# Low parts of the first twelve weight pieces: from GpSimd and VectorE to identity matmuls and ScalarE copies

## The reference, cut to what matters

```python
def _L0_xattn_ref(h, adj_raw, Wq, Wk, gamma_raw):      # h: context, adj_raw: layernorm(x)
    Q = (h @ Wq.T).reshape(b, n, H, d).transpose(0, 2, 1, 3)
    K = (h @ Wk.T).reshape(b, n, H, d).transpose(0, 2, 1, 3)
    sim = jnp.einsum('bhnd,bhmd->bnm', Q, K) / (jnp.sqrt(jnp.float32(d)) * H)
    k = max(1, int(n * TOP_K_RATIO))
    threshold = jax.lax.top_k(sim, k)[0][:, :, -1:]
    A_learned = jax.nn.sigmoid(sim) * (sim >= threshold)
    A_learned = (A_learned + jnp.swapaxes(A_learned, -1, -2)) * 0.5
    gamma = jax.nn.sigmoid(gamma_raw)
    return (1.0 - gamma) * adj_raw + gamma * A_learned
...
x = x + jnp.tanh(g_xattn[0]) * _L0_xattn_ref(ctx_512, _layernorm(x), Wq, Wk, gamma_raw)
xf = _layernorm(x).reshape(-1, C)
y, g = jnp.split(xf @ shared_gw.T, 2, axis=-1)
shared = jax.nn.silu(g) * y @ shared_dw.T
...
x = x + jnp.tanh(g_ffn[0]) * (shared + out)
```

## Time and profile before

| | us |
|---|---|
| median of 3 runs | 598.53 (596.35 to 601.9) |
| profiled execution, its own time | 597.36 |
| its span, first to last instruction | 595.3 |
| mean granted clock of TensorE | 0.937 of full |
| busy: TensorE, VectorE, ScalarE, GpSimd | 505.0, 343.4, 262.7, 231.9 |

### The profile page before, as it was taken

One profiled execution on the slowest core, in us unless ns is written; L12 is line 12 of the kernel. 1 busy time (PEld: TensorE's weight loads), 2 busy tenths in 40 slices (PEclk: granted clock), 3 DMA queues, 4 the chain that ended last, 5 costly groups with the idle time before them and its releaser, 6 DMA issues.

```text
span 595.3 us, 11124 instructions
## 1 busy us (share of the span) xinstructions
PE 505.0 (85%) x3169; PEld 287.2 (48%) x3170; DVE 343.4 (58%) x708; ACT 262.7 (44%) x473; POOL 231.9 (39%) x226
## 2 busy tenths in 40 slices
PE   2302588889998999879998799999999999999992
PEld 0100344444443454444464356666666666666661
DVE  0589758787868786977964477433333333333331
ACT  0696588646774678433231255322322222222221
POOL 1147735462446334540223034344344343343322
PEclk9955779989999999987999899999999999999997
DMA  3236293215610561054005778535435445445433
GB/s 114 95 93 185 78 305 94 57 41 187 237 45 29 169 248 50 29 186 166 0 1 165 235 230 210 95 73 87 91 71 89 88 72 91 84 73 96 77 40 49
DMA packets 33200, 65.84 MB, mean 111 GB/s; under 512 B 4176, under 2 KB 4432, under 8 KB 33168
## 3 DMA queue, kind: packets, MB, share of 16 engines
q1 hardware_dynamic: 24432, 44.99, 23.2%
q0 software_dynamic: 8736, 20.45, 19.1%
HBM read 42.10 MB, written 23.33 MB: 110 GB/s over the span
## 4 chain that ended last, share of the span: by engine, by line
PE 58%; DVE 18%; ACT 7%; issue 6%; DMA 6%; POOL 2%; SPq 1%; DVEq 1%; POOLq 0%; ACTq 0%
PE py L1006 12%; PE pg L986 12%; PE pu L987 12%; PE pg L848 5%; PE pu L848 5%; PE pt_bank L807 4%; DVE w L1180 3%; DVE pa L1139 3%; DVE w L1110 2%; PE pa L996 2%; PE pu L865 2%; DVE w L1143 1%; ACT w L619 1%; DVE w L1187 1%; ACT w L613 1%
## 5 line engine op out<-in xcount | busy, mean ns | idle before, releaser
L986 PE MATMUL pg<-w,x_t 128*128 x468 | 141.9, 315 | 3.8 <-DVE x_t L1442 3.8
L987 PE MATMUL pu<-w,x_t 128*128 x468 | 141.9, 315 | 0.0
L541 POOL DMA_INDIRECT out<-rows,idx x39 | 61.8, 1584 | 138.0 <-ACT rows L747 134.0
L1006 PE MATMUL py<-w,work 128*128 x351 | 82.1, 379 | 0.8 <-DVE work L1437 0.8
L848 PE MATMUL pg<-w 128*128 128x512 f16 (+1 forms) x288 | 79.9, 387 | 2.6 <-DVE work L1233 2.6
L848 PE MATMUL pu<-w 128*128 128x512 f16 (+1 forms) x288 | 79.5, 386 | 0.0
L737 ACT ACTIVATE work<-pg 128x352 f32<-128x352 f32 x39 | 18.1, 463 | 132.5 <-PE pu L987 132.5
L580 ACT ACTIVATE w<-stage 128x544 f16<-128x544 f32 (+1 forms) x80 | 51.0, 647 | 38.8 <-DMA stage<-in_weights 38.4
L488 POOL TENSOR_TENSOR w<-stage,w 128x544 f16<-128x544 f32 (+1 forms) x43 | 53.4, 1250 | 27.4 <-ACT stage L584 25.6
L494 POOL TENSOR_TENSOR work<-work 128x512 f16<-128x512 f32 (+1 forms) x24 | 29.0, 1208 | 81.8 <-ACT work L649 81.8
L1426 DVE SCALAR_TENSOR_TENSOR work<-pu,work 128x352 f32<-128x352 f32 x39 | 20.5, 525 | 65.4 <-ACT work L737 65.4
(11 more groups left out here) (187 smaller groups left out, 756.5 us busy)
## 6 DMA issues: line engine op xcount, KB each, us to landing
stage<-in_weights SPq DMA_DIRECT2D x80, 272.0 KB, 3.6
out<-rows SPq DMA_DIRECT2D x17, 256.0 KB, 5.3
w<-in_x SPq DMA_DIRECT2D x4, 1024.0 KB, 6.8
out<-w SPq DMA_DIRECT2D x16, 256.0 KB, 3.1
xn_rows<-w SPq DMA_DIRECT2D x16, 256.0 KB, 5.5
rows<-out SPq DMA_DIRECT2D x16, 256.0 KB, 2.8
w<-in_ctx_t SPq DMA_DIRECT2D x4, 256.0 KB, 3.6
out<-rows,idx POOLq DMA_INDIRECT x39, 4.8
```

What stands on the lines that cost most here:

```text
L541: pool.indirect_dma_start(out=out, out_offset=bass.IndirectOffsetOnAxis(ap=idx[:, t:t + 1], axis=0), in_=rows[:, t % 2, :], in_offset=None ...
L986: pe.matmul(pg[p][:, 0:H], lhs, w[:, item, half, at:at + H], start=begin, stop=end)
L987: mm = pe.matmul(pu[p][:, 0:H], lhs, w[:, item, half, at + H:at + 2 * H], start=begin, stop=end)
L1006: mm = pe.matmul(py[:, :], hid_t[:, p, part * JC + j, :], w[:, item, half, at:at + C], start=(j, part, half) == (0, 0, 0), stop=(j, part) ...
```

## The change

Low parts of pieces 0 to 11 are made by TensorE: for each half of a piece (272 columns) an fp32 matmul of a diagonal matrix of 256 with the staged fp32, less an fp16 matmul of the identity with the high part, summed in one of four PSUM banks. ScalarE copies each half out as the fp16 low part, and so releases the stage buffer; it no longer scales those pieces in place. Low parts from piece 12 on in items 0 to 2 are all GpSimd's (VectorE makes none of them), and they stand later in its order. TensorE's ten first low parts come ahead of `missed_rows(0)`, the two last behind the projection of batch 1. ScalarE's pieces 16 and 17 lie between the copies of q and k and the normalised rows. TensorE's single wait for the first 16 pieces becomes waits in front of the shared pieces and the down products that read them. Cut to its core:

```diff
+BY_PE = 12
+        low_banks = [py, pu[0], pt_bank, pg[0]]
+        HALF_W = CHUNK_W // 2
...
         def by_dve(item, n):
-            if not isinstance(item, int):
-                return False
-            if item >= LATE:
-                return True
-            return n % RING == RING - 1 and (item >= EARLY - 1 or item * CHUNKS + n < BY_DVE)
+            return isinstance(item, int) and item >= LATE
+
+        def by_pe(item, n):
+            return isinstance(item, int) and item * CHUNKS + n < BY_PE
...
@@ GpSimd
+            c.mark(pool.memset(scaled_ident[:], 0.0))
+            c.mark(pool.memset(minus_ident[:], 0.0))
...
-            for m in (ident, ident16):
+            for m, one in ((ident, 1.0), (ident16, 1.0), (scaled_ident, W_SCALE), (minus_ident, -1.0)):
...
-            first_pieces(0, FIRST)
             add_attention(0)
-            first_pieces(FIRST, FIRST + 3)
+            first_pieces(BY_PE, BY_PE + 1)
             row_scalars(0)
-            first_pieces(FIRST + 3, FIRST + 6)
+            first_pieces(BY_PE + 1, BY_PE + 4)
             guess(1)
             o.clear()
-            first_pieces(FIRST + 6, BEFORE * CHUNKS)
+            first_pieces(BY_PE + 4, BEFORE * CHUNKS)
...
@@ ScalarE
-                if not by_dve(item, n):
+                if not by_dve(item, n) and not by_pe(item, n):
                     after(act, w_hi, item * CHUNKS + n + 1)
                     act.activation(stage[:, n % RING, :], stage[:, n % RING, :], ACT.Copy, scale=W_SCALE).then_inc(w_scaled, 1)
+            def low_from_bank(k):
+                at = k % CHUNKS * CHUNK_W
+                for half in range(2):
+                    after(act, low_mm, k * 2 + half + 1)
+                    act.activation(w[:, k // CHUNKS, 1, at + half * HALF_W:at + (half + 1) * HALF_W],
+                                   low_banks[(k * 2 + half) % 4][:, 0:HALF_W], ACT.Copy).then_inc(w_lo[k % RING] if half else low_sb, 1)
...
-                high_piece(n // CHUNKS, n % CHUNKS)
+                high_piece(0, n)
+                if n >= 2:
+                    low_from_bank(n - 2)
             base(0, (TPB - 1,))
-            for k in range(ROUNDS, FIRST + RING):
+            for k in range(ROUNDS, BY_PE):
+                low_from_bank(k - 2)
                 high_piece(k // CHUNKS, k % CHUNKS)
-            scores_and_rows(0, True, range(FIRST + RING, FIRST + RING + 2))
-            for k in range(FIRST + RING + 2, BEFORE * CHUNKS):
+            for k in range(BY_PE - 2, BY_PE):
+                low_from_bank(k)
+            for k in range(BY_PE, HALVES * CHUNKS):
+                high_piece(k // CHUNKS, k % CHUNKS)
+            scores_and_rows(0, True, range(HALVES * CHUNKS, HALVES * CHUNKS + 2))
+            for k in range(HALVES * CHUNKS + 2, BEFORE * CHUNKS):
                 high_piece(k // CHUNKS, k % CHUNKS)
...
@@ TensorE
+            def low_pieces(begin, end):
+                for k in range(begin, end):
+                    at = k % CHUNKS * CHUNK_W
+                    after(pe, w_hi, k + 1)
+                    for half in range(2):
+                        bank_, lo, hi = low_banks[(k * 2 + half) % 4], half * HALF_W, (half + 1) * HALF_W
+                        if k >= 2:
+                            if half:
+                                after(pe, w_lo[(k - 2) % RING], (k - 2) // RING + 1)
+                            else:
+                                after(pe, low_sb, k - 1)
+                        pe.matmul(bank_[:, 0:HALF_W], scaled_ident[:], stage[:, k % RING, lo:hi], start=True, stop=False)
+                        pe.matmul(bank_[:, 0:HALF_W], minus_ident[:], w[:, k // CHUNKS, 0, at + lo:at + hi],
+                                  start=False, stop=True).then_inc(low_mm, 1)
+            def pieces_ready(n):
+                for r_, s in enumerate(w_lo):
+                    after(pe, s, len(range(r_, n, RING)))
+                after(pe, w_hi, n)
...
+                if 0 in ks and off == 0:
+                    pieces_ready(half * CHUNKS + -(-UP_W // CHUNK_W))
...
+                if 0 in pieces and i == 0:
+                    pieces_ready(HALVES * CHUNKS)
...
             pe.wait_ge(const_ok, 2)
+            low_pieces(0, BY_PE - 2)
             missed_rows(0)
             project(1, None)
+            low_pieces(BY_PE - 2, BY_PE)
+            after(pe, w_lo[(BY_PE - 1) % RING], (BY_PE - 1) // RING + 1)
             turn_attention(0)
             for i in range(TPB):
                 scores(1, i)
             for i in range(TPB):
                 turn_batch(0, i)
-            for s in w_lo:
-                after(pe, s, HALVES * (CHUNKS // RING))
-            after(pe, w_hi, HALVES * CHUNKS)
...
```

More of the change, by code:

```diff
@@ L19 @@
 BEFORE = 3
-FIRST = 14
-BY_DVE = 20
+BY_PE = 12
 KEEP = int(SEQ * 0.3)
@@ L129, in build @@
         ident, ident16 = sb("ident", [P, P]), sb("ident16", [P, P], F16)
+        scaled_ident, minus_ident = sb("scaled_ident", [P, P]), sb("minus_ident", [P, P], F16)
         ones, tri = sb("ones", [P, P], F16), sb("tri", [P, P], F16)
@@ L206, in build @@
         w_scaled = sem("w_scaled")
+        low_mm, low_sb = sem("low_mm"), sem("low_sb")
         x_ld, ctx_ld = sem("x_ld"), sem("ctx_ld")
@@ L253, in scaled_pieces @@
         def scaled_pieces(item, n):
[L254 to L257, removed]
+            return item * CHUNKS + n + 1 - BY_PE
         ROWS_DVE = BATCHES * (TPB - 1)
@@ L428, in _ @@
             c.wait()
-            for m in (ident, ident16):
-                c.mark(pool.affine_select(out=m[:], in_=m[:], compare_op=ALU.not_equal, fill=1.0, base=0,
+            for m, one in ((ident, 1.0), (ident16, 1.0), (scaled_ident, W_SCALE), (minus_ident, -1.0)):
+                c.mark(pool.affine_select(out=m[:], in_=m[:], compare_op=ALU.not_equal, fill=one, base=0,
                                           pattern=[[-1, P]], channel_multiplier=1))
@@ L1153, in count_missed, with masks @@
                 o.then(dve.tensor_reduce(thr[:], hot8, AX.X, ALU.add))
-            def masks(b, piece=None):
+            def masks(b):
                 after(dve, miss_mm, b + 1)
                 o.then(dve.tensor_copy(missed_i[:], pa[0][0:1, 0:1]))
-                if piece is not None:
-                    low_piece(*piece)
                 any_missed = dve.value_load(missed_i[0:1, 0:1], min_val=0, max_val=P * TPB)
@@ L1201, in attended @@
                 dve.sem_inc(ln_stats, 1)
-                if shared is None:
-                    low_piece(HALVES, 3)
                 if shared is not None:
@@ L1248, in _ @@
                 search(0, n)
-            low_piece(0, 3)
             thresholds(0, (0, 1))
-            low_piece(0, 7)
             thresholds(0, (2, 3))
             count_missed()
-            masks(0, (1, 3))
-            low_piece(1, 7)
+            masks(0)
             attended(0, True, None)
```

## The result

The changed kernel takes 612.61 us (median of 4, 610.11 to 613.73), the kernel before 598.72; the ratio is 1.0219, 95% interval 1.0185 to 1.0253. The page: busy shares and the granted clock in 40 slices.

A forecast was written before the change was run, and what follows sets the result against it. TensorE's gap-free start was taken as the bound, set by GpSimd's low part 18 through SP's queue to batch 1's x. 13.5 + 1.8 + 0.2 = 15.5 on 597.4 gave 612.9, 614 on the median; 8-in-10 range 606 to 621.

The forecast's parts named there:

- (b): Count rounds on VectorE: first L1139 at 40.3 instead of 42.67, four cost 2.7 not 5.7, missed count ready near 47.
- (c): TensorE's ten low parts precede the missed-rows matmul, 2.4 each at half clock, 1.2 at full; matmul at 51.5, 2.0 earlier.
- (d): Missed rows to statistics of attended tiles: 2.2 gained without VectorE's low parts; masks stay 5.7, statistics at 64.1.
- (e): ScalarE's pieces 16 and 17 precede normalised rows, load 17 waits for low part 13: rows at 71.5, 1.1 lost.
- (f): GpSimd's low part 18 falls behind batch 1's guess, 13.7 later; x at 100.7, TensorE resumes at 107.3, 13.5 later.
- (g): TensorE idles some 14 us behind batch 0's first two shared pieces, then restarts at half clock, costing 1.8 (0 to 2.5).
- (h): Readiness waits before TensorE's shared pieces and first down group, 60 in four batches: 0.2.
- From there all as before, only shifted: After TensorE's idle stretch and half-clock restart in batch 0, the remaining timeline is unchanged except for the shift.
- the first: Rival: TensorE's clock doesn't rise during the head's low parts; missed rows at 56.7, everything 5 later, 619; chance 0.18.
- The second: Rival: same order, smaller; stores and x take 11, masks 2 shorter, restart free; 9 slower, 607.5; chance 0.17.
- The third: Rival: faster; early counts help, batch 1's x load isn't held, TensorE starts about 4 sooner, 594.5; chance 0.08.
- the fourth: Rival: order as forecast, but slack makes up the delay of batch 1 to within 1%; chance 0.07.

The follow-up runs named there:

- e5: Changed kernel with TensorE's readiness waits put back to one set for 16 pieces ahead of batch 0's router product; 612.26 us, ratio 1.0220.
- e7_unrolled: Changed kernel with TensorE's loop over batches 0 and 1 written out, same work; 612.09 us, ratio 1.0214.
- e7_warm: Changed kernel with TensorE's loop written out and 58 unused matmuls filling its gap behind shared piece 1 of batch 0; 612.94 us, ratio 1.0230.
- e2: Changed kernel with ScalarE's pieces 16 and 17 moved behind the normalised rows and scores of batch 1; 608.06 us, ratio 1.0152.
- e1: Changed kernel with SP's weight loads 20 to 22 moved behind batch 0's stores and the load of batch 1's x; 600.96 us, ratio 1.0022.
- e6: Kernel before the change with SP's weight loads 20 to 22 moved behind the load of batch 1's x; 599.84 us, ratio 1.0022.
- e12: Changed kernel, queues reordered, one wait set, missed rows behind eight low parts, tile stores behind load 16, row stores behind loads 22 and 23; 593.68 us, ratio 0.9914.
- e8: Changed kernel with loads 20 to 22 behind x, ScalarE's pieces 16 and 17 behind the rows, and one set of readiness waits; 597.61 us, ratio 0.9973.
- e3: Changed kernel with loads 20 to 22 behind the load of x and ScalarE's pieces 16 and 17 behind the rows; 599.20 us, ratio 1.0009.
- e9: Changed kernel with SP, ScalarE and GpSimd orders laid out anew (x ahead of row stores and loads 22, 23) and one wait set; 597.73 us, ratio 0.9983.

## Why the prediction was right

The forecast was 614 and 612.6 was measured; the steps behind it can be laid beside the trace. The agreement is good to about 1 us and not to a few tenths: the four profiles that share the change's queues (the changed kernel, e5, e7_unrolled and e7_warm) have TensorE resume at 106.46 to 108.25.

(a) Constants: nothing, as said. The head of this profiled execution is 1.4 late at VectorE's first count all the same (29.86 against 28.48). The load ahead of it and the first scores' clock differ, other runs of the same head lie on both sides (first statistics of x between 24.0 and 26.5), so I take it for chance.

(b) Count rounds: first L1177 at 41.32 where 40.3 was said; with the 1.4 of chance the gain is 2.7 for a predicted 2.4. Four L1177 took 2.60 for a predicted 2.7. The missed count was ready at 48.3, where near 47 was said.

(c) TensorE ahead of the missed rows: 52.47 for 51.5, no more than that late head. The clock had risen for the third low part, fallen in a pause of 1.8 (the part at 41.11 is slow), and risen again near 44. The price of a low part was 2.40 and 1.14 for 2.4 and 1.2. VectorE did wait for it, 3.87.

(d) Missed rows to statistics of tiles: 12.5 (52.5 to 65.0) for 12.6. That is two misses that cancel: the masks took 4.76 and not the 5.7 said, while from their end to the statistics it took 6.15, 0.75 less than before (6.90) where 1.6 was said. (e) Row scalars at 67.14, load 17's high part at 71.52, rows at 72.77: 5.6 behind the scalars, 5.4 said. That this wait and the two pieces' work cost time, e2 shows: 4.5 us.

(f) Guess at 82.69 for 82.1; low part 18 done at 87.75 for 86.9; x at 100.93 for 100.7; TensorE at 107.52 for 107.3. Without the late head of 1.4 these would have come up to 1.4 sooner, so their closeness is in part luck. From low part 18 to x took 13.2 for 13.8. That SP's queue carries the cost, e1 shows: 11.7 of 13.9 us, and e6 shows that there is nothing to gain from its order without the late low parts.

(g) The restart was mis-sized. It was there and slower than I priced it (four groups took 5.03 from start to start, against 2.63 in the kernel before: 2.4), but its worth was nothing, not 1.8. "The attention steps that VectorE does next are laced behind shared products, so it is on the path" is where it went wrong: VectorE's own chain, not the shared products, releases the missed-rows matmul of batch 1, and in the kernel before TensorE had stood 2.38 us in front of that matmul, slack enough to swallow it; in the changed kernel 0.48 of that is left.

```profile
120.65 0.19 PE L794 MATMUL pa<-one,missed 128*1 128x1 f32 x2 [2.38 <-DVEq L1151]
```

The Trainium skill (TensorE: Matmul & The Clock Gate, Part 1) puts the ramp's penalty under 1% of a typical kernel span. Here 2.4 us is 0.4% where it happens, and e7_warm shows that none of it reached the end, because of that wait and not because the ramp was small.

(h) Waits: nothing that can be seen; 0.2 was said.

"From there all as before, only shifted" didn't hold, and the sum has no term for it. From batch 1's attention transposes to batch 3's it took 122.55 and 122.56 us in the two profiles without the change (before and e6), and 124.04 to 124.86 in all twelve with it: 1.5 to 2.3 more (1.8 in the changed kernel). In the changed kernel a part is seen behind batch 1's transposes. TensorE stood 2.46 in front of them, not 1.04; the granted clock then was 0.57 from 143.4 to 147.1, and the projection ran at half clock, so that batch 2's statistics of x began 0.7 later behind the transposes than before. The rows of the kernel before, then of the changed one:

```profile
128.69 1.06 PE L802 MATMUL pa<-ident,w 128*128 128x128 f32 x8 [1.04 <-DVE w L1180]
...
130.46 1.02 PE L782 MATMUL pu<-w 128*128 128x512 f32 x2
```

```profile
141.95 1.06 PE L816 MATMUL pa<-ident,w 128*128 128x128 f32 x8 [2.46 <-DVE w L1216]
...
144.28 1.91 PE L796 MATMUL pu<-w 128*128 128x512 f32 x2
```

In e1 and e12 that projection is at full clock and VectorE waits 1.88 and 1.65 for batch 2's x instead, so no single cause is shown. The readiness waits aren't it, for e5 and e8 to e12 have one set of them and a loss of the same size (1.5 to 2.3).

The sum without (g) is 13.7 and the difference of the medians 13.9 (13.1 by the ratio); the full sum of 15.5 was made for the profiled execution, where the difference is 16.0. Two wrong terms cancel in it: 1.8 for a restart that cost nothing, and nothing for the batches, which took 1.8 more. So the mechanism was right up to TensorE's resumption, and the last us or two of the forecast were luck.

The rivals: the clock did rise, so the first is out. The second wasn't wholly wrong: of its three savings the restart came true, the masks gave 0.9 of its 2, and low part 18 to x took 13.2 where it wanted 11; it falls because the largest of them, 2.8 in the queue, didn't come (0.6 did). The third needed another reading of the queues, and e1 confirmed mine; the fourth fell with TensorE's resumption: over the thirteen versions the time follows it nearly one to one (13.8, 7.9, 2.0, -1.7 and -5.5 us against the kernel before's 93.77 go with +13.9, +8.9, +1.8, +0.1 and -4.4 us; e8 is furthest off, by 2.6).

e3's median is 1.8 us worse than its resumption says. In its profile batches 1 to 3 are where the head start went: 124.41 from transposes to transposes against 122.55. What stays open is the cause of that loss, which no run separates, and why some medians don't show it (e9 gains 1.9 where its resumption says 1.1). The granted clock at the later transposes varies too (eight took 1.65 in the changed kernel's batch 2, 1.06 before). Nor was the full order of e12 tried without TensorE's low parts, so how much of its 4.4 us is the order's and how much the head start's isn't shown; e6 shows only that moving loads 20 to 22 is worth nothing there.

## What to carry to other kernels

Work moved later on one engine is moved past everything that stands in front of it in every other engine's queue: before taking low parts 16 to 18 behind a wait, find the queue whose entries they release (SP's buffers here) and what else is queued behind those entries. The relief itself was real (statistics of batch 0's tiles at 65.0 with a head 1.4 late, against 68.2), and the kernel came out 4.4 us ahead in e12, where stores and loads stand in the order in which they are waited for and the missed rows come earlier. And a slow restart of TensorE is to be priced at its next wait for another engine, not where it happens. Last, whether the rest is only shifted has to be measured, over a later stage, between the same two marks in both profiles.

## What the runs showed of the hardware

- A low part on TensorE (two fp32 matmuls and two fp16 ones of 272 columns) took 2.40 us at half clock (41.11) and 1.14 at full clock; a ScalarE copy of 272 fp32 PSUM columns took 0.37, and 0.28 from one start to the next.
- The granted clock fell in a pause of 1.83 us (39.3 to 41.1, 0.79 over 39 to 42, 0.50 over 42 to 44), although in the kernel before it held over one of 1.79 ahead of 93.77. The engine had been busy without a stop for 12 us there, and with pauses here.
- The same instruction of VectorE with two SBUF inputs (L1139 of the kernel before, 128x512) took 0.70 us with GpSimd idle and up to 1.77 with GpSimd's subtractions beside it. The Trainium skill (SBUF — State Buffer, SBUF: two separate sides) calls this an exclusive lock, held for the whole instruction. The trace agrees: the excess of 1.07 is no longer than one subtraction of 1.22.
- A weight load of 272 KB landed 7.2 us behind its issue when the load of x and four row stores shared the DMA engines (e9), and 2.69 us behind it when they didn't.
